# GpSimd adds the value bias per tile, x is loaded ahead of a block move, and ScalarE evacuates in another order

## The reference

```
h = relu(layernorm(x))
q, k, v = h Wq' + bq, h Wk' + bk, h Wv' + bv
weight = adj * exp(q k');  weight = weight / rowsum(weight)
x1 = x + weight v                                  # layer 0
g = relu(layernorm(x1))
agg = (adj g) / max(rowsum(adj), 1e-6)
out = x1 + relu([g, agg] W1')                      # layer 1
```

## Time and profile before

| | us |
|---|---|
| median of 3 runs | 2059.47 (2041.43 to 2060.54) |
| the profiled execution | 2038.23 |
| its span, first to last instruction | 2036.4 |
| TensorE matmul busy | 1983.7 (97%) |
| VectorE busy | 1309.0 (64%) |
| GpSimd busy | 889.0 (44%) |
| ScalarE busy | 778.2 (38%) |

### The profile page before, as it was taken

One profiled execution on the slowest core, in us unless ns is written; L12 is line 12 of the kernel. 1 busy time (PEld: TensorE's weight loads), 2 busy tenths in 40 slices (PEclk: granted clock), 3 DMA queues, 4 the chain that ended last, 5 costly groups with the idle time before them and its releaser, 6 DMA issues.

```text
span 2036.4 us, 28198 instructions
## 1 busy us (share of the span) xinstructions
PE 1983.7 (97%) x9356; PEld 1655.3 (81%) x9356; DVE 1309.0 (64%) x2329; ACT 778.2 (38%) x1289; POOL 889.0 (44%) x958
## 2 busy tenths in 40 slices
PE   8799999999999999999999999999999999999999
PEld 6688888888888888888888888888888878878887
DVE  5665666666667666666666666656676656666654
ACT  3333433333433434443334333334334343333432
POOL 2354444444444444444445444444444444344530
PEclk9899999999999999999999999999999999999999
DMA  4324333333434244334343333344342333424321
GB/s 160 114 99 129 129 104 128 112 114 129 126 106 134 99 128 129 113 108 137 100 134 124 113 113 124 102 132 127 98 136 99 127 118 103 129 93 134 124 73 42
DMA packets 162369, 236.47 MB, mean 116 GB/s; under 512 B 14768, under 2 KB 111024, under 8 KB 162352
## 3 DMA queue, kind: packets, MB, share of 16 engines
q1 hardware_dynamic: 162352, 236.25, 35.8%
HBM read 137.63 MB, written 98.57 MB: 116 GB/s over the span
## 4 chain that ended last, share of the span: by engine, by line
PE 41%; DVE 22%; issue 13%; DMA 9%; POOL 7%; ACT 5%; SPq 2%; DVEq 0%; POOLq 0%; ACTq 0%
PE bank L361 14%; PE bank L363 13%; PE bank L362 13%; DMA turned<-turned_store 4%; DVE h L786 4%; DMA turned_store<-blocks 4%; DVE x L871 4%; DVE stats L750 3%; POOL gT_l L305 3%; DVE w L844 3%; SPq L212 2%; POOL w_l L187 2%; DVE deg L774 2%; DVE blocks L730 2%; DVE y L856 1%
## 5 line engine op out<-in xcount | busy, mean ns | idle before, releaser
L305 POOL TENSOR_TENSOR gT_l<-turned,gT_h 128x512 fp32r<-128x512 f32 x124 | 157.4, 1291 | 302.4 <-ACT gT_h L608 302.4
L305 POOL TENSOR_TENSOR hT_l<-turned,hT_h 128x512 fp32r<-128x512 f32 x124 | 183.0, 1497 | 186.9 <-ACT hT_h L577 186.9
L856 DVE SCALAR_TENSOR_TENSOR y<-bank,deg_inv,y 128x512 f32<-128x512 f32 x128 | 96.1, 750 | 217.0 <-PE bank L363 215.5
L361 PE MATMUL bank<-wb_h,gT_h 128*128 128x512 f32 x496 | 197.4, 398 | 29.5 <-DVE kz_l L726 29.5
L361 PE MATMUL bank<-hT_h,n_h 128*128 128x512 f32 x512 | 201.2, 393 | 10.0 <-POOL hT_l L305 10.0
L617 ACT ACTIVATE y<-bank 128x512 f32<-128x512 f32 x128 | 76.6, 598 | 335.4 <-PE bank L363 335.4
L726 DVE TENSOR_TENSOR kz_l<-bank,kz_h 128x512 fp32r<-128x512 f32 x128 | 88.5, 691 | 176.5 <-ACT kz_h L562 176.5
L362 PE MATMUL bank<-hT_l,n_h 128*128 128x512 f32 x512 | 200.9, 392 | 0.0
L363 PE MATMUL bank<-hT_h,n_l 128*128 128x512 f32 x512 | 200.7, 392 | 0.0
L602 ACT ACTIVATE kz_h<-bank,kp_bias 128x512 fp32r<-128x512 f32 x128 | 87.7, 685 | 295.2 <-PE bank L363 291.2
L361 PE MATMUL bank<-wv_h,hT_h 128*128 128x512 f32 x512 | 199.6, 390 | 0.0
(11 more groups left out here) (125 smaller groups left out, 4777.8 us busy)
## 6 DMA issues: line engine op xcount, KB each, us to landing
turned_store<-blocks SPq DMA_DIRECT2D x124, 512.0 KB, 2.7
turned<-turned_store SPq DMA_DIRECT2D x496, 128.0 KB, 2.8
x_in<-x SPq DMA_DIRECT2D x32, 1024.0 KB, 6.0
out<-x SPq DMA_DIRECT2D x124, 256.0 KB, 2.0
adjT<-adj_t SPq DMA_DIRECT2D x32, 512.0 KB, 3.5
w<-adj SPq DMA_DIRECT2D x32, 512.0 KB, 4.6
x<-wq SPq DMA_DIRECT2D x4, 256.0 KB, 4.0
xb<-wk SPq DMA_DIRECT2D x4, 256.0 KB, 4.4
```

Source lines behind the costliest of these rows:

```text
L305: pool.tensor_tensor(by_blocks(dst, t), turned_tile(t), by_blocks(high, t).bitcast(F32), ALU.subtract).then_inc(done, 1)
L361: pe.matmul(dst, lh, rh, start=first, stop=False)
L856: nc.vector.scalar_tensor_tensor(out=y[:, :], in0=bank[L1_BANK + 1][:, :], scalar=deg_inv[:, t:t + 1], in1=y[:, :], op0=ALU.mult, op1=ALU. ...
```

## The change

Four orders are changed; no arithmetic is added or removed.

- SyncE: in a step with both layers, x of pair i + 1 is loaded before the store and load of graph 0 of g, and no longer after them.
- GpSimd: `add_bv` works tile by tile, each tile waiting for its own tile of x1 of pair j only; the two graphs of `scale_and_shift(1, j)` come after the second and after the third tile.
- ScalarE: `exp(0)` comes ahead of `high_gT(0)` and `high_gT(1)`.
- ScalarE: `high_z(0)` comes ahead of `next_h(0)` and `next_h(1)`, and `high_z(1)` ahead of `next_h(2)` and `next_h(3)`.

```
--- before.py
+++ after.py
@@ -237,13 +237,12 @@
 
             def step(i, layer0=True, layer1=True, more=True):
                 j = i - 1
-                if layer0 and layer1:
-                    store_blocks(1, 0, g_turned, T * j + NT, g_stored)
-                    load_turned(1, 0, g_stored, j + 1, g_moved)
                 if layer1 and more:
                     sp.wait_ge(xb_done, T * (i + 1))
                     load_x(i + 1)
                 if layer0 and layer1:
+                    store_blocks(1, 0, g_turned, T * j + NT, g_stored)
+                    load_turned(1, 0, g_stored, j + 1, g_moved)
                     store_blocks(1, 1, g_turned, T * (j + 1), g_stored)
                     load_turned(1, 1, g_stored, j + 1, g_moved)
                 if not layer1:
@@ -280,9 +279,9 @@
             pool.wait_ge(ident_done, 1)
             pool.tensor_scalar(diagonal[:, :], ident[:, :], -1.0, None, ALU.mult).then_inc(diagonal_done, 1)
 
-            def scale_and_shift(n, i):
-
-                for g in range(G):
+            def scale_and_shift(n, i, graphs=range(G)):
+
+                for g in graphs:
                     tiles = slice(NT * g, NT * g + NT)
                     pool.wait_ge(moments_done[n], 2 * (G * i + g + 1))
                     pool.tensor_tensor(rs[n][:, 0, tiles], var_eps[n][:, tiles], minus_half[:, :],
@@ -294,10 +293,10 @@
                     pool.tensor_tensor(rs[n][:, 1, tiles], mean_sum[n][:, tiles], half_rstd[n][:, tiles],
                                        ALU.mult).then_inc(shift_done[n], 1)
 
-            def add_bv(i):
-                pool.wait_ge(x_loaded, 16 * (i + 1))
-                for t in range(T):
-                    pool.tensor_tensor(xb[:, t, :], x_in[:, t, :], bv_b[:, :], ALU.add).then_inc(xb_done, 1)
+            def add_bv(i, t):
+                if t == 0:
+                    pool.wait_ge(x_loaded, 16 * (i + 1))
+                pool.tensor_tensor(xb[:, t, :], x_in[:, t, :], bv_b[:, :], ALU.add).then_inc(xb_done, 1)
 
             def low_tile(dst, high, t, high_done, count, done):
 
@@ -322,11 +321,15 @@
                 if not layer0:
                     return
                 if layer1:
-                    scale_and_shift(1, j)
-                    pool.wait_ge(x1_done, T * i)
-                add_bv(i)
-                if not layer1:
-                    scale_and_shift(0, i + 1)
+                    for t in range(T):
+                        pool.wait_ge(x1_done, T * j + t + 1)
+                        add_bv(i, t)
+                        if t > 0:
+                            scale_and_shift(1, j, range(t - 1, min(t, G)))
+                else:
+                    for t in range(T):
+                        add_bv(0, t)
+                    scale_and_shift(0, 1)
                 if layer1:
                     low_gT(j, 0)
                     low_gT(j, 1)
@@ -657,10 +660,10 @@
                         high_weight(2)
                         act.wait_ge(weight_split, 3)
                     high_v(0)
+                    exp(0)
                     if layer1:
                         high_gT(0)
                         high_gT(1)
-                    exp(0)
                     exp(1)
                     high_w(0)
                     if layer1:
@@ -669,16 +672,17 @@
                     high_w(1)
                     for t in range(1, T):
                         high_v(t)
+                if layer1:
+                    high_z(0)
                 if more:
                     next_h(0)
                     next_h(1)
                 if layer1:
-                    high_z(0)
+                    high_z(1)
                 if more:
                     next_h(2)
                     next_h(3)
                 if layer1:
-                    high_z(1)
                     high_z(2)
                 if layer0:
                     act.wait_ge(w_summed, G * (i + 1))
```

## The result

| | before | changed |
|---|---|---|
| median, us | 2058.74 (4 runs, 2041.43 to 2060.54) | 1997.79 (4 runs, 1997.02 to 1998.77) |
| profiled execution, us | 2038.23 | 1997.02 |
| its span, us | 2036.4 | 1995.2 |

The ratio is 0.9722, with a 95% interval of 0.9663 to 0.978. The forecast was 2000 us, in a range of 1988 to 2040. Between the two profiled executions the span fell by 41.2 us; the sum had said 40.8. The distances between the starts of neighbouring matmuls, added up by place, put 41.1 of it at the start of z(2) and inside z(2).

A forecast was written before the change was run, and what follows sets the result against it. TensorE, busy 97%, was held by one gap per pair at z(2). Gaps 36.5 plus fallen clock 4.3 give 40.8 off 2038.23, 1997.4 us; with half of z(3)'s pessimistic bound 2000, range 1988 to 2040.

The forecast's parts named there:

- The gap and its price: TensorE's wait for kz_l at z(2), once per pair: 29.5 us idle, a gain of 36.5 us with the added costs.
- 0.24 for each of 29 gaps: At z(2), each gap costs its idle time plus 0.16 + 0.08 = 0.24 us.
- The pitch of 60.7: From one pair's z(2) to the next, 60.7 us once the gap is gone.
- The clock: TensorE's clock falls to 1.2 GHz behind long gaps; the falls cost 2.7 and 1.6 us, 4.3 to be regained.
- the 21 us: Median above profiled execution; taken as later x transfers acting through the gap, so gone with it; otherwise 2019 us.
- x ahead of the store: On SyncE, x issued six microseconds earlier; graph 0 of g later by 3 us, graph 1 earlier by 1.6.
- the late pair's 9.95 us: Time from x's issue until the store behind it landed in a late pair of the kernel before, not 7.26.
- exp first: exp(0) ahead of graph 0's copies on ScalarE: 0 us; exp(1) keeps a slack of 2.6 us to v(3).
- z(3), the next in line: z(3) needs low_z(1), behind next_h: slack 1.2 us; only late pairs wait, 3 to 4 us in all as pessimistic bound.
- The adds' 0.7 per pair: GpSimd's adds by tile delay VectorE's small sum and what follows: 0 to 0.7 us per pair, taken as 0.
- The first: Rival: the wait moves to z(3), which takes over part of the gap; 2018 us, or 2039 on the median's scale; 15%.
- the third: Rival: slower, v(3) waits for exp(1) behind graph 0's copies, behind x; 2073 us with 12.5 us for x and store; 5%.

The follow-up runs named there:

- before_again: The kernel before, unchanged, run for a second trace: 2038.41 us, ratio 1.0027; its profiled execution took 2032.45 us.
- exp_first_only: The kernel before with only exp(0) moved ahead of high_gT(0): 2039.62 us, ratio 0.9978.
- z_only: The kernel before with only ScalarE's new order of high_z(0) and high_z(1): 2002.95 us, ratio 0.9844.
- early_start: The changed kernel with h of pair 1 made earlier in step 0, by ScalarE's next_h and VectorE's turn of graph 0: 1991.37 us, ratio 0.9726.

## Why the prediction was right

**The gap and its price.** Shown. The sum of idle time and 0.24 for each of 29 gaps, with the fallen clock, was 40.8; the span gave 41.2, and 41.1 of that stood at z(2). The pitch of 60.7, the 1.2 us ahead of z(2) and the 1.2 ahead of z(3) were met to 0.1.

**The clock.** In the changed kernel every stretch from 90 us on has a granted clock of 1.00; the two falls went with their gaps.

**The median.** The prediction had the 21 us between the profiled execution and the median go along with the gap, for want of another source. That came true: the changed kernel's executions lie within 1.8 us of one another, where the kernel before spread from 2027 to 2066 over all the runs. before_again and exp_first_only fit that their lengths follow the kz_l wait (25.8 us at 2032.45, 29.5 at 2038.23, 39.4 at 2049.11). The 21 us themselves belong to this set, since the later sets had medians of 2038 to 2048; had the kernel before been at 2038 here too, the forecast of 2000 would have been the same.

**x ahead of the store.** Against the unhindered z(2) (1038.04 before) x was issued 18.2 us ahead of it and is now issued 24.3 ahead (1084.70 less 1060.36, z(2) being one pitch of 60.68 after 1024.02). Graph 1's copy stands 8.26 ahead, computed at 8.24; graph 0's copy 13.5 ahead, computed at 12.7 to 14.7. The slack of exp(1) to v(3) is 3.5 (1012.41 to 1015.86) and not 2.6. In the pairs from step 2 on, the copies stand 12.6 to 13.8 and 7.1 to 8.4 ahead, so the latest pair has the slack that was computed.

What the prediction did not foresee is that x itself becomes steadier. It had reckoned with the late pair's 9.95 us for x and store also in the new place. In the changed kernel's trace these two never take more than 7.1. The page of the kernel before and that of the changed kernel give for x, 1024 KB, the middle time from issue to landing:

```profile
x_in<-x SPq DMA_DIRECT2D x32, 1024.0 KB, 6.0
...
x_in<-x SPq DMA_DIRECT2D x32, 1024.0 KB, 5.3
```

In the six traces in which x is issued behind the loads of graph 0, it lands after 5.8 to 9.0 us; in the six in which it is issued ahead of them and nothing is added, after 5.0 to 6.1. In the old place the DMA engines are still 83% busy when x is issued (1019 to 1020 us of the trace before), in the new one they are idle (1058 to 1060 of the trace after). That the place makes the difference is shown; that the overlap with the loads is the reason is not.

**What was mis-sized or mis-placed.** The prediction gave all 36.5 us to the order of high_z and to x only slack. By the runs either suffices in an ordinary pair, and x is the better of the two: with the adds and exp first it has all of the gain (1996.39), the order of high_z alone leaves 5 us (2002.95). The least sound step is "z(3), the next in line". Its bound of 3 to 4 us was meant for DMAs that come no earlier than now, which is z_only, and the 3.8 us idle there agree with it partly by luck: in late pairs z(2) waits already, since ScalarE is held at high_gT(2) in front of high_v and high_z(0), and more is lost there (3.3 us) than at z(3) (2.7). In the changed kernel neither place waits. exp first was put at 0 us; with the old order of high_z it is worth 9 (2005.44 to 1996.39). The adds' 0.7 per pair (0.5 by the small sum's 0.16 and 0.69) was rightly held to be hidden in the changed kernel, and is a loss of 0.8% where the gap is open.

**The rivals.** The first and the third are real mechanisms, at z(3) and at v(3), and did not decide for want of delay: 3.5 us more in front of graph 0 brings up the one and a little of the other, 2 MB the other in every pair.

## What to carry to other kernels

Follow a gap of the busiest engine back through the in-order queues to the transfer that starts the chain, and note at each queue what stands ahead of the instruction without being needed by it. Here, moving that transfer forward, into a stretch where the DMA engines are idle, cured the usual gap and its jitter; moving the last link forward cured only the usual gap. The price of the first is paid by what now queues behind the transfer (graph 0 comes 2.5 us later), so its slack has to be worked out. An edit that costs nothing under cover can cost its full delay where the gap is open, so parts are to be judged together and not one by one. When executions of a kernel differ by 2%, an exposed transfer of uneven length is a thing to look for.

## What the runs showed of the hardware

From issue to landing, a 0.5 MB store with nothing queued ahead of it took 2.7 us and, once, 5.2 (early_start), with the DMA engines 4% busy near the end. A 1 MB load took 5.0 to 6.1 us in one place of the step and 5.8 to 9.0 in another. A VectorE sum of 128x2 from SBUF took 0.69 us and not 0.16 beside GpSimd's adds.

The executions of the kernel before varied by 1.9%, and its two longest gaps cost 2.7 and 1.6 us in fallen clock on top of themselves; the executions of the kernel without the gap varied by 0.1%. That late transfers are what makes the whole spread is argued from the traces above, not shown for the longest executions.
